# A graph layer in three passes: x times its first weight is made in f32 in the filing stage and read back later, x's low half comes from TensorE, and each adjacency row has 49 blocks in place of 50

## The reference

```python
def _graph_conv(x, edges, W0, b0, W1, b1):
    src = jnp.concatenate([edges[:, 0], edges[:, 1]])
    dst = jnp.concatenate([edges[:, 1], edges[:, 0]])
    deg = jnp.maximum(jax.ops.segment_sum(jnp.ones_like(dst, dtype=x.dtype), dst, num_segments=N_NODES), 1.0)
    agg = jax.ops.segment_sum(x[src], dst, num_segments=N_NODES) / deg[:, None]
    return x @ W0 + b0 + agg @ W1 + b1

xn = _layernorm(x)
h  = relu(_graph_conv(xn, edges, W0_0, b0_0, W1_0, b1_0))      # 256 -> 512
g  = _graph_conv(h, edges, W0_1, b0_1, W1_1, b1_1)             # 512 -> 256
x  = x + g + mix(xn)          # linear attention, d = 256, 8 heads
x  = x + ffn(_layernorm(x))   # 8 experts, the best 2 of each node
```

## Time and profile before

| what | value |
|---|---|
| runs | 2358.42, 2359.82, 2360.38 us; median 2359.82 us |
| the profiled execution, its own time | 2360.88 us |
| its span, first to last instruction | 2359.4 us |
| mean granted TensorE clock | 0.935 of 2.4 GHz |
| PE, DVE, ACT, POOL busy | 2110.9, 1578.0, 1196.6, 371.0 us |
| filing, 37 to 378 us | PE busy 201.57 us, DVE 303.45 us, clock 0.68 |
| first pass, 415 to 1122 us | PE busy 702.16 of 707 us |
| hidden stage, 1122 to 1434 us | PE busy 301.56 of 312 us |
| second pass, 1434 to 1981 us | PE busy 541.85 of 547 us |

### The profile page before, as it was taken

How to read it: one execution, slowest core, us unless ns; L and a number is a source line. 1 busy time by engine, 2 the same in 40 slices (tenths; PEclk the granted TensorE clock), 3 DMA queues, 4 the chain that set the end, 5 groups by cost and what they waited for, 6 DMA issues and landing times.

```text
span 2359.4 us, 53463 instructions
## 1 busy us (share of the span) xinstructions
PE 2110.9 (89%) x15342; PEld 1308.3 (55%) x15343; DVE 1578.0 (67%) x4938; ACT 1196.6 (51%) x2432; POOL 371.0 (16%) x436
## 2 busy tenths in 40 slices
PE   2556567999999999999899999999999997799997
PEld 2444444555555555555455554444444443699996
DVE  6999997899999999999343433444445445355554
ACT  2456553555555555555455552444444443466664
POOL 2000000000000000000110111112111212366665
PEclk9666667999999999999899999999999998899998
DMA  3111114422222222222121215555555554655553
GB/s 82 41 40 45 39 38 140 141 117 117 111 114 117 111 116 114 111 111 111 70 103 51 82 56 199 190 205 192 186 198 203 188 187 161 173 93 92 91 92 46
DMA packets 131007, 275.62 MB, mean 117 GB/s; under 512 B 30479, under 2 KB 83904, under 8 KB 128756
## 3 DMA queue, kind: packets, MB, share of 16 engines
q1 hardware_dynamic: 103411, 221.23, 27.0%
q0 software_dynamic: 25856, 47.15, 9.2%
q10 hardware_dynamic: 1664, 6.35, 0.8%
HBM read 137.14 MB, written 132.95 MB: 114 GB/s over the span
## 4 chain that ended last, share of the span: by engine, by line
PE 80%; DVE 8%; DVEq 4%; issue 3%; DMA 2%; ACT 1%; POOL 1%; ACTq 0%; SPq 0%; POOLq 0%
PE bank L2154 45%; PE bank L2145 6%; PE bank L2375 6%; PE bank L2360 6%; PE bank L2307 5%; PE bank L2295 5%; PE bank L2310 2%; PE bank L2342 1%; DVEq L1051 1%; DVE big L1054 1%; DVE big L1067 1%; DVEq L1063 1%; PE bank L2162 1%; DMA big<-rows_dram 1%; DVE big L1065 1%
## 5 line engine op out<-in xcount | busy, mean ns | idle before, releaser
L2154 PE MATMUL bank<-RW,big 128*128 128x512 f16 (+1 forms) x4900 | 1180.0, 380 | 5.3 <-DMA big<-a_dram 5.0
L2154 PEld LDWEIGHTS bank<-RW,big 128*128 128x128 f16 x4900 | 443.7, 98 | 401.8 <-issue 9.2
L1814 ACT ACTIVATE big<-bank 128x512 f16<-128x512 f32 (+1 forms) x640 | 371.7, 581 | 317.7 <-PE bank L2145 317.7
L1209 DVE TENSOR_TENSOR big<-iotaB,keys 128x512 f16<-128x512 f16 x1300 | 452.0, 417 | 7.9 <-issue 7.8
L2145 PEld LDWEIGHTS bank<-big 128*128 128x128 f16 x2560 | 190.8, 98 | 111.6 <-DVE big L1209 1.1
L2145 PE MATMUL bank<-big 128*128 128x128 f16 x2560 | 247.2, 219 | 0.7 <-DVE big L1209 0.7
L916 POOL DMA_INDIRECT out_dram<-big x112 | 181.2, 1618 | 111.5 <-ACT big L1971 77.5
L852 POOL DMA_DIRECT2D big<-in_L_ffn_W_dram x8 | 6.4, 801 | 1107.9 <-DVE R L1268 1105.2
L1962 ACT ACTIVATE big<-bank,b1A,iscA 128x256 f32<-128x256 f32 x224 | 114.1, 560 | 98.9 <-PE bank L2360 91.9
L2375 PE MATMUL bank<-RW,big 128*128 (+1 forms) x1344 | 156.9, 274 | 0.0
L2360 PE MATMUL bank<-big,RW 128*128 128x256 f16 x1344 | 156.3, 273 | 0.4 <-ACT big L1951 0.4
(11 more groups left out here) (397 smaller groups left out, 2996.5 us busy)
## 6 DMA issues: line engine op xcount, KB each, us to landing
big<-a_dram SPq DMA_DIRECT2D x49, 832.0 KB
big<-a_dram SPq DMA_DIRECT2D x49, 768.0 KB, 4.6
a_dram<-big SPq DMA_DIRECT2D x49, 640.0 KB, 2.9
a_dram<-big SPq DMA_DIRECT2D x49, 512.0 KB, 2.6
a_dram<-big SPq DMA_DIRECT2D x49, 448.0 KB, 2.5
big<-rows_dram SPq DMA_DIRECT2D x56, 265.0 KB
big<-in_x_dram SPq DMA_DIRECT2D x96, 128.0 KB, 2.1
big<-in_L_ffn_W_dram POOLq DMA_DIRECT2D x16, 512.0 KB, 4.7
```

The costliest lines, as they stand in the source:

```text
L1209: last = v.tensor_tensor(out[q].rearrange("p b (m k) -> p b m k", k=2), inturn(iotaB[:, :], QB, P // 2), twice(kd[:, q * QB:(q + 1) * QB, ...
L1814: a.activation(Ab[q][:, 0:n], banks[BB(q)][:, 0:n], ACT.Copy).then_inc(s_ab, 1)
L2154: last = mm(bank[:, :], blk(q, c), src, start=(u == 0), stop=(u == T))
```

## The change

It has three parts.

1. x times W0 moves from the hidden stage to the filing stage. ACT now writes the transposed tiles in pairs (`xst`), and PE multiplies them by W0 in f32 (`own1`: per call 4 matmuls of 256 columns; one call for each tile, and 2 of half the width at the end). ACT copies the product out of PSUM (`xown`, 128 x 512), SP stores it to DRAM (`own_dram`) and reads it back in the hidden stage, one part ahead of its use. There PE adds up 6 matmuls in place of 12, DVE adds the stored product (`added4`), and only then ACT takes the ReLUs, now from SBUF. `xhigh4` and `xlow4` fall away, and half of the work that cuts W0 and W1 into halves.
2. In the filing stage the low half of x comes from PE: one f32 matmul with an identity times S and one f16 matmul of the high half with minus the identity, both into the free half of bank 5; `low` on DVE falls away, and ACT reads the low half from PSUM. To free bank 7, the Gram matrix's second half is cut to its upper part (129 columns in place of 257) and the missing corner is transposed from the first half at the end. 
3. A row of adjacency has 49 blocks: the tables' last column is exchanged, so that the block of the tile itself and the edges kept apart are built into one. `apply` is 49 matmuls in both passes, the stored rows are narrower, and PE's loops over the tiles of both passes are written out.

```diff
-ABLK = T + 1
+ABLK = T
@@ PE, filing
                 pe.wait_ge(s_xtc, t + 1)
+                pe.wait_ge(s_xlo, t + 1)
                 for h in range(2):
                     nc.tensor.transpose(banks[5][:, h * P:(h + 1) * P], xs[:, h * P:(h + 1) * P], ident[:, :])
-                for h in range(2):
-                    last = mm(banks[6 + h][:, 0:D + 1], xs[:, h * P:(h + 1) * P], xs[:, 0:D + 1],
-                              start=False, stop=False)
-                last.then_inc(s_xt, 1)
+                mm(banks[6][:, 0:D + 1], xs[:, 0:P], xs[:, 0:D + 1], start=False, stop=False)
+                mm(banks[6][:, D + 1:2 * D + 2 - P], xs[:, P:D], xs[:, P:D + 1], start=False, stop=False)
+                mm(banks[5][:, D:2 * D], identS[:, :], xs[:, 0:D], start=True, stop=False)
+                pe.wait_ge(s_xhi, t + 1)
+                mm(banks[5][:, D:2 * D], minus16[:, :], R2[:, t * 2 * D:t * 2 * D + D], start=False, stop=True)\
+                  .then_inc(s_xt, 1)
+
+            def own1(i):
+
+                pe.wait_ge(s_xe, i) if i else pe.wait_ge(s_w, 16 * 16)
+                pe.wait_ge(s_xtc, min(i // 2 * 2 + 2, T) + 1)
+                n = P if i >= T - 1 else 2 * P
+                for c in range(2):
+                    f = i % 2 * 2 + c
+                    for k in range(2):
+                        last = mm(banks[7][:, c * n:(c + 1) * n], W0s[:, k, f * P:(f + 1) * P],
+                                  xst[i // 2 % 2][:, k, 0:n], start=(k == 0), stop=(k == 1))
+                last.then_inc(s_xw, 1)
...
                 gram(t)
+                if t >= 2:
+                    own1(t - 2)
                 file1(t, t % 2)
@@ ACT, filing
                 a.activation(R2[:, bass.ds(t * 2 * D, D)], xs[:, 0:D], ACT.Copy, scale=S).then_inc(s_xhi, 1)
+                if t >= 3:
+                    own1(t - 3)
                 if t + 1 < T:
                     deviation1(t + 1)
                 place1(t)
-                act.wait_ge(s_xl, t + 1)
-                a.activation(R2[:, bass.ds(t * 2 * D + D, D)], xlo, ACT.Copy, scale=S).then_inc(s_xlo, 1)
+                a.activation(R2[:, bass.ds(t * 2 * D + D, D)], banks[5][:, D:2 * D], ACT.Copy, scale=S).then_inc(s_xlo, 1)
@@ DVE, filing
                 ranks(t, t % 2)
-                low(t)
@@ DVE, the turn, behind the joining of the tables
+            dve.drain()
+            for i, tab in enumerate((tv, uv)):
+                v.tensor_copy(lastc[:, i, :], tab[:, :, T - 1])
+            dve.drain()
+            for tab, out in ((TT, tv), (TU, uv)):
+                v.tensor_copy(out[:, :, T - 1], tab[:, 0:(T - 1) * TC + T:TC + 1])
+            dve.drain()
+            for i, tab in enumerate((TT, TU)):
+                v.tensor_copy(tab[:, 0:(T - 2) * TC + T - 1:TC + 1], lastc[:, i, 0:T - 1])
@@ SP, hidden stage
+            for g in range(1, T // W):
+                for h in range(2):
+                    sp.wait_ge(s_hl, (g - 1) * 8 + 4 * h + 4)
+                    load_own(g, h)
+                if g + 1 < T // W:
+                    sp.wait_ge(s_yp, (g + 1) * W)
+                    load4(g + 1, (g + 1) % 2)
@@ DVE, hidden stage
+            def added4(g, j):
+                h, f = j // 4, j % 4
+                if f == 0:
+                    dve.wait_ge(s_own[h], g * (16 * (h + 1)) + 16 * (h + 1))
+                dve.wait_ge(s_hp, g * 8 + j + 1)
+                v.scalar_tensor_tensor(out=h4[j], in0=banks[f][:, 0:n4[h]], scalar=hsc2, in1=h4[j],
+                                       op0=ALU.mult, op1=ALU.add).then_inc(s_ha, 1)
...
-                low4(g)
+                added4(g, 0)
+                for j in range(1, 8):
+                    added4(g, j)
+                    low4(g, j - 1)
+                low4(g, 7)
@@ ACT, hidden stage
-                        act.wait_ge(s_hp, g * 8 + j + 1)
+                        act.wait_ge(s_ha, g * 8 + j + 5)
...
-                        act.wait_ge(s_hl, g * 8 + j + 1)
-                        a.activation(hhi4[:, f, t0 * P:(t0 + tn) * P], banks[f][:, 0:tn * P], ACT.Relu,
-                                     bias=sbh[:, f:f + 1], scale=hsc2)
+                        a.activation(hhi4[:, f, t0 * P:(t0 + tn) * P], h4[j], ACT.Relu,
+                                     bias=sbh[:, f:f + 1], scale=hsc)
@@ PE, hidden stage
-                        pe.wait_ge(s_hr, g * 8 + j + 1)
+                        pe.wait_ge(s_ha, g * 8 + j + 1)
...
-                        for k in range(4):
+                        for k in range(2):
@@ PE, apply and the loops
-                    u = q * QB + c
-                    src = R2[:, u * 2 * D:(u + 1) * 2 * D] if u < T else R2[:, bass.ds(t * (2 * D), 2 * D)]
-                    last = mm(bank[:, :], blk(q, c), src, start=(u == 0), stop=(u == T))
+                    i = q * QB + c
+                    u = t if i == T - 1 else T - 1 if i == t else i
+                    last = mm(bank[:, :], blk(q, c), R2[:, u * 2 * D:(u + 1) * 2 * D], start=(i == 0), stop=(i == T - 1))
...
-                with pe.Fori(0, T // 2) as k:
-                    tile1(2 * k + 1, banks[7])
-                    tile1(2 * k + 2, banks[5])
+                for t in range(T):
+                    tile1(t, banks[7 if t % 2 else 5])
```

More of the change, by code:

```diff
@@ L836, in _ @@
                 pool.wait_ge(s_xT[1], 16 * (T // 2))
+                for i in range(2):
+                    pool.wait_ge(s_xo[i], 16 * ((T + 1) // 2))
                 overflow(0)
@@ L1447, in _ @@
                 dve.wait_ge(s_xT[1], 16 * (T // 2))
+                for i in range(2):
+                    dve.wait_ge(s_xo[i], 16 * ((T + 1) // 2))
                 overflow(0, rd1)
@@ L1781, in _ @@
             act.wait_ge(s_pm, 4)
-            for i in range(2):
-                last = a.activation(Gs[:, i, :], banks[6 + i][:, 0:D + 1], ACT.Copy)
-            last.then_inc(s_vm, 1)
+            a.activation(Gs[:, 0, :], banks[6][:, 0:D + 1], ACT.Copy)
+            a.activation(Gs[:, 1, P:D + 1], banks[6][:, D + 1:2 * D + 2 - P], ACT.Copy).then_inc(s_vm, 1)
+            own1(T - 1)
+            own1(T)
+            act.wait_ge(s_gt, 1)
+            a.activation(Gs[:, 1, 0:P], banks[7][:, 2 * P:3 * P], ACT.Copy).then_inc(s_gc, 1)
             act.wait_ge(s_pm, 5)
@@ L2224, in tile1 @@
                         degrees(t)
-                    if q == 11 and last:
+                    if q == 11 and t:
                         transposed(t - 1)
@@ L2256, in tiles2 @@
                 tile2(2, 0, 1, (1, 1), (0, 0), banks[5])
-                with pe.Fori(1, T // 2) as k:
+                for k in range(1, T // 2):
                     tile2(2 * k + 1, 1, k, (2 * k, 0), (2 * k - 1, 1), banks[7])
```

276 lines of the change are left out of this document (148 added, 128 removed).

## The result

The changed kernel takes 2326.46 us (median of 4 runs, 2321.24 to 2328.0), the kernel before 2359.19 (median of 4 on the same chip): ratio 0.9857, 95% interval 0.984 to 0.9874. The profiled execution took 2325.6 us, span 2324.1, against 2360.9: 35.3 us less where 39 were predicted. By the medians it is 32.7 us less, 5.5 us above the 2321 us of the prediction.

The account below looks back on a forecast made before the run. PE bounds three stages, DVE filing. Filing +19, turn +3, POOL's start +1, passes -21 and hidden stage -41 sum to -39 us: 2322 us for the profiled execution, 2321 for the median; 8-in-10 range 2298 to 2350.

Parts of the forecast that it names:

- A tile of 5.6 us in filing: Filing: a tile takes 5.6 us at 2.4 GHz, 0.33 us more than now, though DVE is relieved.
- PE's chain: Filing: PE's own work and wait per tile, 3.5 us before and 5.6 us with the change at 2.4 GHz.
- the ring: Filing: cycle of waits through ACT, DVE and PE, 4.98 us a tile before, 5.55 with the product's emptying.
- PE's 0.89 us gap: Filing: PE's wait for L1718 in each tile, counted in its tile time and called its only gap.
- 49 x 0.33 = +16, -9 and -1: +6: Filing: 49 tiles 0.33 us longer, less 9 for DVE's longer work using idle time, less 1 for halved weights.
- 2.1 us for each of 6 restarts, +13: Filing: after each `prepare` PE runs at 1.2 GHz for 5 us, costing 2.1 us each, 13 us in all.
- The rival of a clock low throughout: Filing: PE's clock stays low, tiles take 9.9 us, +150 us in place of +19, total 2452 us; chance 8%.
- Turn +3 (2 to 6): Between filing and first pass: three more `own1` and ACT's copies add 3 us; DVE's column exchange is covered.
- Two passes -21: First and second pass: one matmul less a tile, 0.217 us each, 49 tiles, twice; written-out loops cost 0.
- Hidden stage -41: Hidden stage: `hidden` takes 11.2 us in place of 18.16, -6.8 us a group, six groups; range -55 to -31.
- the chain: Hidden stage: DVE free 4.5 us after PE's start, first addition 5.2, four ReLU pairs 10.5, fourth subtraction 11.2 us.
- ACT's four pairs: Hidden stage: ACT's pairs of ReLUs start every 1.3 us; all four done at 10.5 us after PE's start.

Follow-up runs that it names:

- a4: Changed kernel with ACT's emptying of the product moved behind the next tile's deviation in filing: 2358.58 us, ratio 0.9989.
- a3: Changed kernel with ACT's filing order changed: normalized tile, high half and next deviation first, then the PSUM copies and product emptying: 2290.72 us.
- b0: Changed kernel plus 80 filler f16 matmuls on PE in each of six stretches of filing where PE waits for DVE's `prepare`: 2311.44 us.
- a1: Kernel before with only 49 blocks in place of 50, the column exchange and PE's tile loops written out: 2343.05 us, ratio 0.9924.
- c2: On c1, DVE and ACT do the first group's sums before the first expert's weights, and split each expert later: 2280.30 us.
- b1: Changed kernel with the next expert's weights split behind a group's fourth tile, not its fifth, on ACT and DVE: 2322.62 us.
- b2: Changed kernel without DVE's addition in the hidden stage; ReLUs read PSUM directly and x's product is left out of the output: 2316.87 us.
- c1: On a3, the hidden stage's ACT writes a tile's low half after the next tile's high half, and takes norms one tile later: 2275.73 us.
- b3: Changed kernel with the edits of a3 and b1 together: 2288.89 us, ratio 0.9704.

## Why the prediction was right, step by step

- **A tile of 5.6 us in filing**: right, 5.53. But the reason was half right. I gave PE's chain and the ring the same length; a4 shows that they share ACT's queue, so that one cannot be shortened by lengthening the other, and a3 that PE's 0.89 us gap, which I took as given, and the copies in the ring could go together.
- **"49 x 0.33 = +16, -9 and -1: +6"**: an ordinary tile of before is not 5.27 but 5.35 on average (117.7 us for 22), as PE at 1.2 GHz now and then set the pace. These 22 steps grew by 4.0 us, the 8 long ones shrank by 4.4, the 6 `prepare` by 1.8, and the 12 steps behind a `prepare` are 1.1 us dearer even without the slow clock: -1 in place of +6.
- **"2.1 us for each of 6 restarts, +13"**: right. The 12 steps behind a `prepare` grew by 15.3 us, 1.1 of it counted above; 2.2 to 2.7 us above 5.50 + 5.53 for each, 14.2 in all. b0 took 11.0 of filing away, and the 14.2 but for the 3 us that its filling cost where it outlasted the `prepare`. Filing: +13.3 where +19 stood. The rival of a clock low throughout did not come: 0.89 in the mean.
- **Turn +3 (2 to 6)**: +6.1 in this execution, just past the end of its range. The exchange is free (a1). I had worked out the turn without PE's clock, and the clock is what varies in it. Mean granted clock and length of the turn in kernels that all have the change: 0.80 and 51.3 us (the changed kernel), 0.80 and 50.6 (a3), 0.80 and 50.4 (c2), 0.87 and 48.7 (b0), 0.90 and 47.5 (b1, b2), 0.86 and 47.1 (c1), 0.94 and 45.1 (b3). With b1's clock the turn would have cost +2.3. A second thing that I did not name does not vary: near the last tiles SP's queue holds the store of a product behind the last rows of x, ACT waits for it to empty the next (2.5 us here, 2.3 to 2.4 in b0, b1 and b2), and PE for ACT. Before, ACT waited 1.8 us there for the last rows of x. Two pieces of the chain that ended last (start, us, what):

```profile
381.15 5.37 DMA own_dram<-big
...
387.25 2.50 PE bank L2100 x8
```

- **Two passes -21**: -19.7. The second gave its 0.217 a tile; the first is 1.8 us short of it, 2.3 in a1, in its first tile and by 0.02 to 0.03 us a tile in its later half. The first tile is the clock again: here four `apply` matmuls still take 1.87 us at 434.68, where before four take 1.03 at 413.36, and the tile is 15.84 us long in place of 14.84. In b3, where the clock is up after the first four, it takes 14.68 us and the whole pass 695.0. The written-out code triples the packets of the instruction queue (100 against 34) without a wait of PE on it; whether the 0.03 us come from it stays open.
- **Hidden stage -41**: -35.0. The first group gained nothing (33.7 against 33.3), as predicted; PE's row of the timeline, with an idle time of 18.55 us in it:

```profile
1160.39 5.55 PE L2365 MATMUL bank<-R,RW 128*128 x24 [18.55 <-DVE big L1548]
```

  In the steady groups the chain was right link by link: DVE free after 4.4 us (4.5 predicted), first addition done after 5.1 (5.2). The term mis-sized is ACT's four pairs, 5.8 us in place of 5.3, and 0.4 of small steps: 12.1 in place of 11.2. Most of the 0.5 is the 0.10 us a pair that a source in SBUF costs, which I had named and left out of the sum. The second group is the other miss: 13.9 us, a saving of 4.3 and not 6.8, with the start's backlog in it.
- The sum came within 4 us because the errors cancel, which is luck: filing 6 too dear, the hidden stage 6 too good, the turn 3 too cheap, the passes 1 too good, and 1.5 us less at the seams and behind them.

## What to carry to other kernels

When an engine becomes the limit, look at its remaining gap before its work: PE's 0.89 us in each filing tile, and with them 33 us of filing, hung on the order of a few small instructions in ACT's queue. A handover to and fro between two engines (1.92 us for 0.9 us of work each) stays hidden until the third engine is made faster; overlap it by one item first, and only then move long work around it. And make the ledger from several executions of like code: b1's whole gain of 4 us lay in a stretch that the edit did not touch, where only the clock differed.
